# Feed-forward weight units turned by VectorE in 32 by 32 squares, thirty of them made during cross-attention

## What is computed

```python
# causal attention, 16 heads of 128
q = einsum('bsd,hed->bhse', x, W_Q)      # k, v alike
scores = where(causal, -1e9, q @ k^T * scale)
out = einsum('bhse,hde->bsd', softmax(scores) @ v, W_O)

# feed-forward: I = 2048, H = 512
def _mx_dequant(t):                       # blocks of 32 along the last axis
    scales = maximum(max(abs(blocks)) / 448, 1e-30)
    q = (blocks / scales).astype(float8_e4m3fn).astype(float32)
    return q * scales
gate = _mx_dequant(x) @ _mx_dequant(gate_w).T          # up alike
out = _mx_dequant(silu(gate) * up) @ _mx_dequant(down_w).T
```

## Time and profile before

| | |
|---|---|
| median of 3 runs | 2578.45 us (2575.19 to 2582.25) |
| the profiled execution | 2577.9 us |
| its span | 2575.9 us |
| mean granted TensorE clock | 0.964 of full |
| TensorE busy | 2296.5 us, 89% |
| VectorE busy | 1755.0 us, 68% |
| ScalarE busy | 1220.8 us, 47% |
| GpSimd busy | 588.2 us, 23% |
| DMA | 184.84 MB, mean 72 GB/s |

### The profile page before, as it was taken

The page is one execution under the profiler, slowest core; times in us unless marked ns, Lnnn a source line. Parts: engine busy times, 40 slices in busy tenths (PEclk is TensorE's granted clock), DMA queues, the critical chain, the costliest instruction groups (busy, mean ns, idle before and its releaser), DMA issues. The chain is left out here.

```text
span 2575.9 us, 31979 instructions
## 1 busy us (share of the span) xinstructions
PE 2296.5 (89%) x11664; PEld 1568.9 (61%) x11664; DVE 1755.0 (68%) x3374; ACT 1220.8 (47%) x1972; POOL 588.2 (23%) x435
## 2 busy tenths in 40 slices
PE   3779999999999999895897989788888779899998
PEld 2556666666666665564775446555555438677776
DVE  7855776767777678786786775776767754554444
ACT  4443465656656566633343114576766853211111
POOL 7710033333333333440000002414132300000000
PEclk9889999999999999997899999999999989899999
DMA  3331101000000100004443100000000014556661
GB/s 131 115 139 37 33 21 29 9 29 9 29 29 9 37 9 13 1 1 175 161 178 145 71 21 10 1 6 5 6 5 1 21 59 158 200 209 223 234 234 67
DMA packets 47062, 184.84 MB, mean 72 GB/s; under 512 B 6272, under 2 KB 11136, under 8 KB 36672
## 3 DMA queue, kind: packets, MB, share of 16 engines
q1 hardware_dynamic: 46912, 182.86, 19.7%
HBM read 173.93 MB, written 8.91 MB: 71 GB/s over the span
## 5 line engine op out<-in xcount | busy, mean ns | idle before, releaser
L403 PE MATMUL wide_a<-wide_w,ctxT 128*128 128x256 f32 (+1 forms) x2048 | 437.8, 367 | 2.8 <-POOL wide_eps L372 2.8
L403 PEld LDWEIGHTS wide_a<-wide_w,ctxT 128*128 128x128 f32 x2048 | 368.2, 191 | 76.8 <-issue 35.7
L385 POOL TENSOR_TENSOR wide_sums<-wide_sums,wide_s 128x512 f32<-128x512 f32 x224 | 302.0, 1348 | 458.3 <-ACT wide_s L533 445.1
L428 PE MATMUL wide_scores<-wide_q,wide_keysT 128*128 128x512 f32 x512 | 238.4, 604 | 10.8 <-ACT wide_s L529 10.8
L438 PE MATMUL wide_o<-wide_s,wide_values 128*128 128x512 f32 x512 | 232.5, 597 | 3.5 <-ACT wide_s L533 3.5
L529 ACT COPY wide_s<-wide_scores 128x512 f32<-128x512 f32 x256 | 148.6, 586 | 179.9 <-PE wide_scores L428 168.6
L1830 DVE TENSOR_REDUCE int_peaks<-int_a 128x1 f32<-128x1024 f32 x128 | 156.1, 1222 | 88.4 <-PE int_a L1553 87.2
L1553 PE MATMUL int_a<-int_keys,int_qrows 96*128 96x512 bf16 x512 | 150.0, 390 | 58.1 <-DVE int_peaks L1830 31.4
L1705 ACT ACTIVATE int_prob<-int_a,int_shift,int_qscale 128x1024 uint8<-128x1024 f32 x128 | 155.5, 1216 | 49.9 <-PE int_a L1553 49.4
L428 PEld LDWEIGHTS wide_scores<-wide_q,wide_keysT 128*128 128x128 f32 x512 | 87.9, 189 | 147.1 <-ACT wide_s L529 86.0
L591 DVE TENSOR_TENSOR wide_top<-wide_top,wide_s 128x512 f32<-128x512 f32 x240 | 165.6, 690 | 15.4 <-ACT wide_s L529 9.6
(11 more groups left out here) (426 smaller groups left out, 4240.8 us busy)
## 6 DMA issues: line engine op xcount, KB each, us to landing
moe_gate_up<-hbm_m_gu SPq DMA_DIRECT2D x34, 1408.0 KB, 6.1
moe_down<-hbm_m_down_a SPq DMA_DIRECT2D x34, 512.0 KB, 7.0
causal_wqkv<-hbm_wqkv SPq DMA_DIRECT2D x8, 1536.0 KB, 6.7
ctxT<-hbm_ctxT SPq DMA_DIRECT2D x4, 2048.0 KB, 15.1
oproj_raw<-hbm_wproj SPq DMA_DIRECT2D x8, 1024.0 KB, 5.4
ctxT_again<-hbm_ctxT SPq DMA_DIRECT2D x4, 2048.0 KB, 14.8
moe_down<-hbm_m_down_b SPq DMA_DIRECT2D x34, 192.0 KB, 7.2
wide_unit<-hbm_ffn_units SPq DMA_DIRECT2D x24, 256.0 KB, 2.6
```

The costliest lines, as they stand in the source:

```text
L385: ins = pool.tensor_tensor(sums[0][:, :], before, part[:, j, :], ALU.add)
L403: mm = pe.matmul(a[h][:, j, cols], ctxT[:, kc, t * P:(t + 1) * P], w[g % 2][:, kc, cols], start=(kc == 0), stop=(kc == KC - 1))
L428: pe.matmul(sp_[j % 2][:, :], keysT[:, j, :], q[:, :], start=True, stop=True).then_inc(s_s, 1)
```

## The change

1. The host lays each unit out so that a turn of every 32 x 32 square by itself gives the turned unit (`arrange`). `mx_parts` writes its product to the scratch tile and ends in one new VectorE instruction, `transpose` of 128 x 512. The product stays one instruction.
2. 30 units, not 24, are made in the wide stage, and stored turned. Steps 0 to 8 and step 23 take two halves, and the list ends with steps 60 and 61 instead of 56 and 57.
3. In the causal stage TensorE and ScalarE have nothing to do with units. VectorE makes the 18 that are left, three in each of pairs 0 and 1, two in pairs 2 to 7, straight into `ffn_weights`; the inversion stands between the halves of the first. Four buffers for raw units take the place of four and two.
4. TensorE's order in the causal stage is new: `project_out` is one pair later and stands behind `project(p, 0)`, the turned probabilities stand behind it and behind `project(p, 1)`, the scores at the end.
5. The 30 made units come back by 8 loads: three in pairs 5 to 7, two behind the last pair, three at the start of the feed-forward stage ahead of the context. The feed-forward products wait for six group semaphores.

```diff
+FFN_LATE = [7, 23] + [u + n for n in range(8, 16) for u in (0, 16)]
+FFN_EARLY_UNITS = [n for first in (0, 16, 4, 20, 32, 36, 40, 44) for n in range(first, first + 4) if n not in FFN_LATE]
...
-    slots = [n for n in range(N) if n <= 2 * QPG + 1 or n % QPG not in (2, 3)][:2 * FFN_EARLY]
+    halves_at = [1 if n <= 2 * QPG + 1 or n % QPG not in (2, 3) else 0 for n in range(N)]
+    for n in list(range(QPG + 1)) + [3 * QPG - 1]:
+        halves_at[n] = 2
+    slots = [n for n in range(N) for _ in range(halves_at[n])][:2 * FFN_EARLY]
...
-                    if n in slots:
-                        i, half = divmod(slots.index(n), 2)
-                        (scale_unit, round_unit)[half](i)
+                    for k in [k for k in range(2 * FFN_EARLY) if slots[k] == n]:
+                        (scale_unit, round_unit)[k % 2](k // 2)
...
+    due = [0, 3, 6] + [6 + 2 * n for n in range(1, NP - 1)]
...
+                load_unit(3)
                 for p in range(NP):
-                    for i in range(UP * p + 3, min(UP * p + 3 + UP, FFN_UNITS)):
-                        load_unit(i)
                     if p + 2 < NP:
                         sp.wait_ge(s_p, 3 * p + 3)
                         sp.dma_start(wqkv[p % 2][:, :, :, :], A["wqkv0"][p + 2]).then_inc(s_w[p % 2], 16)
...
+                    if p >= 2:
+                        sp.wait_ge(s_acc, p - 1)
+                        sp.dma_start(wo[p % 2][:, :, :], A["wo0"][p]).then_inc(s_wo[p % 2], 16)
+                    for i in range(due[p], due[p + 1]):
+                        if i + NR < NL:
+                            load_unit(i + NR)
+                    if p >= 5:
+                        load_units(sp, (0, 16, 32)[p - 5], (0, 0, 2)[p - 5])
+                for first in (4, 20):
+                    load_units(sp, first, 1)
...
-                for p in range(NP):
-                    unit(UP * p + 1)
-                    unit(UP * p + 3)
-                    mask_and_peak(p, 0)
-                    mask_and_peak(p, 1)
-                    unit(UP * p + 5)
-                    invert(p, 0)
-                    invert(p, 1)
+                for p in range(NP + 1):
+                    for i in range(due[p], due[p + 1]) if p < NP else ():
+                        scale_unit(i)
+                        if i == due[p] and p >= 1:
+                            invert(p - 1, 0)
+                            invert(p - 1, 1)
+                        round_unit(i)
+                    if p == NP:
+                        invert(p - 1, 0)
+                        invert(p - 1, 1)
+                    else:
+                        mask_and_peak(p, 0)
+                        mask_and_peak(p, 1)
...
+                    if t == 0 and f < 2:
+                        pe.wait_ge(s_group[f], 32)
...
+                    if t == 0:
+                        pe.wait_ge(s_group[2 + f], 16)
...
+                for f in range(1, 4):
+                    load_units(sp, 32 + 4 * f, 2 + f)
                 for kc in range(KC):
                     sp.dma_start(ctxT[:, kc, :], A["ctxT"][:, kc, :]).then_inc(s_ctx, 16)
...
-    A["ffn_units"] = np.concatenate([gate_up, down], 0)
+    units = np.concatenate([gate_up, down], 0).reshape(48, 4, 32, KC, 4, 32)
+    A["ffn_units"] = units.transpose(0, 4, 2, 3, 1, 5).reshape(48, P, DM)
...
-        return dve.tensor_tensor(blocks(out), blocks(raw), spread(stat[:, 1, :]), ALU.mult)
+        link(dve.tensor_tensor(blocks(power), blocks(raw), spread(stat[:, 1, :]), ALU.mult))
+        return dve.transpose(out, power)
```

More of the change, by code:

```diff
@@ L343, in load_unit @@
                         sp.wait_ge(s_stored, 16 * (i - 1))
-                    sp.dma_start(unit[i % 2][:, :], units[2 * i]).then_inc(s_unit[i % 2], 16)
+                    sp.dma_start(unit[i % 2][:, :], units[FFN_EARLY_UNITS[i]]).then_inc(s_unit[i % 2], 16)
                 def store_unit(i):
@@ L361, in _ @@
                             sp.dma_start(w[(g + 1) % 2][:, :, :], wkv_dram[g + 1]).then_inc(s_w[(g + 1) % 2], 16)
-                    if n - 1 in slots[1::2]:
-                        i = slots.index(n - 1) // 2
+                    for i in [i for i in range(FFN_EARLY) if slots[2 * i + 1] == n - 1]:
                         store_unit(i)
@@ L790, in causal_attention_stage @@
         acc = [st.ps(f"acc{t}", [P, DM]) for t in range(NT)]
-        names = "masks proj proj_copied scores masked shift exp inv norm turned kept probT out z acc dequantised dve"
-        (s_mk, s_p, s_pc, s_sc, s_ms, s_sh, s_exp, s_inv, s_norm, s_tp, s_kept, s_pt, s_out, s_z, s_acc, s_deq, s_dve) = (
+        names = "masks proj proj_copied scores masked shift exp inv norm turned probT out z acc rounded dve"
+        (s_mk, s_p, s_pc, s_sc, s_ms, s_sh, s_exp, s_inv, s_norm, s_tp, s_pt, s_out, s_z, s_acc, s_deq, s_dve) = (
             st.sem(n) for n in names.split())
[L795 to L801, removed]
         with nc.Block() as block:
@@ L909, in project_out @@
                         mm.then_inc(s_acc, 1)
-                for p in range(NP + 1):
+                for p in range(NP + 2):
                     if p < NP:
                         project(p, 0)
-                        turn_unit(UP * p)
+                    if p >= 2:
+                        project_out(p - 2, 0)
+                        project_out(p - 2, 1)
+                    if 1 <= p <= NP:
+                        turn_prob(p - 1, 0)
+                    if p < NP:
                         project(p, 1)
-                        turn_unit(UP * p + 1)
+                    if 1 <= p <= NP:
+                        turn_prob(p - 1, 1)
+                    if p < NP:
                         project(p, 2)
-                    if p >= 1:
-                        turn_prob(p - 1, 0)
+                    if 1 <= p <= NP:
+                        weigh(p - 1, 0)
+                        weigh(p - 1, 1)
                     if p < NP:
@@ L1043, in _, with ffn_stage @@
                     dve.tensor_tensor(x[:, t, :], x[:, t, :], acc[t][:, :], ALU.add)
-def ffn_stage(nc, C, x, weights, loads):
+def ffn_stage(nc, C, x, weights, s_group, loads):
     NF = 4
@@ L1177, in build_middle @@
             weights = memory.enter_context(nc.sbuf_tensor("ffn_weights", [P, FFN_UNITS, 4, P], F32))
+            s_group = [nc.alloc_semaphore(f"ffn_units_loaded{n}") for n in range(6)]
             with ExitStack() as inner:
```

112 lines of the change are left out of this document (35 added, 77 removed).

## The result

The changed kernel takes **2565.64 us** (median of 5 runs, 2557.97 to 2566.72) against 2578.45 (5 runs, 2575.19 to 2582.25): a ratio of **0.9933, 95% interval 0.9917 to 0.9949**, a gain of 12.8 us. The profiled execution took 2565.89, its span is 2564.1 at a mean granted clock of 0.961.

A forecast was written before the change was run, and what follows sets the result against it. Both the wide and causal stages were taken to be bound by TensorE. From 2577.9 us, minus 29.3 (causal stage), plus 2.3 and 3.0 (wide stage), came 2553.9, stated as 2554, with a range of 2545 to 2567.

The forecast's parts named there:

- Rival 1: Causal stage: the new order is worth nothing, only the unit turns count, 20.6 us; total 2562.6; chance 0.12.
- Causal stage: 29.3 forecast: Causal stage gains 29.3 us: pairs of 17.05 us instead of 21.2, TensorE still the bound, turned probabilities' wait hidden.
- first wait of 6.5: Causal stage, pair 1: TensorE waits some 6.5 us (before 4.93), then runs one projection at the lower clock.
- second wait, 0.5: Causal stage, after pair 1: VectorE's three units, masks and the rest end late, costing TensorE 0.5 us more.
- The turn at 0.73 with its gap: VectorE's new 128x512 transpose takes 0.73 us with its gap, like an fp32 pass over two tensors (0.69).
- DMA loads at nothing: The 8 loads of made units, each under 5 us, cost nothing; without cover each would be 4.5 us.
- Steps 0 to 8 ... 2.3 us: Wide stage, both halves per step: step 1 is 1.4 us late, then 8 x 0.11 us; cost 2.3 us.
- Steps 9 to 55 ... Cost 0: Wide stage: turns and one more half in step 23 fit VectorE's waits, 1.8 us each in 57 places; cost 0.
- My own sign of being wrong: TensorE idle in the body of the wide stage, where the earlier profile had it without a gap.
- Steps 56 to 63 ... Cost 3.0: Wide stage's end, VectorE the bound: 6.4 us added, less 2 x 1.34 and some 0.7 of gaps; cost 3.0 us.
- Rival 2: VectorE becomes the wide stage's bound: the turn costs 1.64 us everywhere beside GpSimd's adds; total 2569.4; chance 0.07.
- Rivals 3 and 4: 3: turn slow in itself, 2612 at 3.36 us, chance 0.04; 4: units reach feed-forward late, 2557 to 2563, chance 0.05.

The follow-up runs named there:

- second median: The changed kernel run again with no edit: 2567.76 us (12 runs), ratio 0.9962 to the kernel before.
- 24-unit run: Changed kernel with 24 units in the wide stage, one turned half a step, and 24 in the causal stage, three a pair: 2574.24 us, ratio 0.9974.
- short adds: Changed kernel with GpSimd adding 16 of 512 columns in all wide-stage sums but the first of each head group: 2544.43 us, ratio 0.9865.
- old order: Changed kernel with TensorE's and ScalarE's old order in the causal stage, still without the units there: 2570.19 us, ratio 0.9975.
- first with 27 units: Changed kernel with 27 units in the wide stage (two halves in steps 1 to 6, none at step 60), 21 in the causal: 2565.03 us, ratio 0.9944.

## Why the prediction was right, and where it was not

The direction was right and 2565.6 lies in the range, near its upper end; the forecast, 2554, was 11.6 us too low. The gain forecast was 24.4 us; measured three times, it was 12.8, 9.5 and 14.4. That the range held is in part luck: its upper end was there for rivals 1 and 4, which did not come, and what filled it is a loss in the wide stage of 15.8 us where 5.3 were forecast. The second median, 2567.76, lies just outside.

- **Causal stage: 29.3 forecast, 30.8 measured.** The pair of 17.05 us is 17.1; the first wait of 6.5 is 4.89, and the projection behind it, at the lower clock in part, took 4.90 where 5.8 was reckoned; the second wait, 0.5, is 0.74; the turned probabilities have no wait over 0.7 us in the pairs after it; from the last pair's first score to the add it took 13.1 us, reckoned 12.5. TensorE stays the bound at two units a pair, and the 24-unit run shows the other side: at three, VectorE is, at 19.66 us.
- **The turn at 0.73 with its gap: right** (0.711 and a gap). The estimate that I took from the Trainium skill's figures (VectorE: DVE Perf Modes, The three transpose paths), 1.24 us a unit, was too long for this form.
- **DMA loads at nothing: right.** The feed-forward stage took 83.9 us between its first and last gate matmuls, before 83.5, and no DMA ends a wait there. In the wide stage the queue mattered only in variants.
- **"Steps 0 to 8 ... 2.3 us": 3.1.** Its parts are off: steps 2 to 8 cost 0.01 each instead of 0.11, and step 1 3.0 instead of 1.4. I had the late scores right and left out the lower clock that came behind the longer wait.
- **"Steps 9 to 55 ... Cost 0" is the step that failed in kind: 3.8 us.** I argued from the mean wait, 1.8 us in 57 places. That a half turned from scaling to rounding would meet the adds is in no mean. The earlier trace rows had the fact before me (0.69 and 1.64 for one form), and I used it for the new instruction alone, not for the old ones that it moves. My own sign of being wrong, TensorE idle in the body of the stage, came: 1.38 us at 486 and 1.05 us at 530. Step 9's 0.7 us are of another kind: TensorE waits 0.40 us for the first group's peaks (L600), and the loss stays with the short adds and goes without the turn or with single halves there.
- **"Steps 56 to 63 ... Cost 3.0": 6.0**, for the same reason; the runs without the turn and without halves there show the phase, and with the short adds these steps even gain.
- **Not in the sum: 2.9 us between the last turn and the output projection.** It goes with when the clock falls. In the five profiles with 98.9 to 99.3 us (the change three times, the old order, the first with 27 units) the clock is 1.00 in the 11 us behind the last turn, TensorE then waits 1.9 to 2.2 us before the last scores, and the clock is 0.76 in the next 14 us. In the other seven changed kernels and in the kernel before (96.1 to 97.3) it is 0.69 or 0.84 first and 1.00 after. Why it falls earlier or later stays open.

Rival 1 fell, though its 2562.6 lies nearer to the result than my sum: the order is worth something (4.2 us, of which I had no estimate of its own), if not much. Rival 2 named the right neighbours and the wrong victim: beside GpSimd's adds the change lost up to 9 us (3.1 at steps 20 to 25, 6.0 at 60 to 62, gone with the short adds), but not one turn was stretched. Rivals 3 and 4 fell with the rows above.

## What to carry to other kernels

When work is added on an engine that shares something with a neighbour, price not only the new instructions but those that they push into the neighbour's busy time. Average slack does not show that; put both timelines side by side at the periodic places and see which instruction would stand beside what. Where work can be placed in slots, keep the slots that held and add in stretches where the neighbour is idle, and let no wait stand ahead of an unrelated load in a queue.

## What the runs showed of the hardware

The stretching goes by the form of the instruction. Beside GpSimd's adds VectorE's products and sums of two tensors go from 0.69 to 1.64 us and the one-source TENSOR_SCALARs, which take 0.43 us (or 0.29 at 16 bits) for 512 columns and so pass more than one column in the time that a sum needs for one, to 1.3 to 1.5. TENSOR_REDUCE (0.69) and STREAM_TRANSPOSE (0.711) stay as they are; 15 of the 30 turns in the wide stage lay beside the adds nearly from end to end, at 711 to 712 ns like the rest. By the Trainium skill (SBUF - State Buffer, Who interferes with whom) VectorE contends with GpSimd where it has two SBUF inputs or runs in a two-port mode, and the first to start holds the port for its whole instruction. The trace agrees on which are stretched, if the one-source TENSOR_SCALARs are counted as two-port by their rate (0.43 us against 0.69); that a port is held for a whole instruction no row shows by itself.

TensorE's clock at step 1: idle for 1.22 us (turn left out) it went on at 1.98 us for four blocks of 512 columns, idle for 1.94 it took 2.90 and then 4.44 instead of 3.62, the lower of its two levels for part of them. A wait of 0.7 us more cost 2.4.
